# Other groups of query tiles in the index loop of a two-block transformer, VectorE's sums and selections interleaved, one head pair moved behind the loop

## The reference

```python
iq = (hidden_states @ idx_wq_w).reshape(b, s, IDX_H, IDX_D)       # 16 index heads of 128
ik = hidden_states @ idx_wk_w
iw = hidden_states @ idx_weights_w * IDX_H ** (-0.5)
idx_scores = jnp.einsum('bqn,bnqk->bqk', iw, jax.nn.relu(jnp.einsum('bqnd,bkd->bnqk', iq, ik))) * IDX_D ** (-0.5)
idx_scores = jnp.where(causal, idx_scores, -jnp.inf)
_, topk_idx = jax.lax.top_k(idx_scores, TOPK)                     # 128 of up to 1024
...
scores = jnp.where(mask[:, None], scores, -jnp.inf)
attn = jax.nn.softmax(scores, axis=-1)                            # 32 heads
```

## Time and profile before

| | us |
|---|---|
| three runs: median (lowest to highest) | 1416.42 (1415.38 to 1418.27) |
| profiled execution | 1415.27 |
| its span | 1413.5 |
| TensorE busy, of the span | 1308.7 (93%) |
| VectorE busy | 1089.0 (77%) |
| ScalarE busy | 822.2 (58%) |
| GpSimd busy | 715.1 (51%) |

### The profile page before, as it was taken

The page is one execution under the profiler, slowest core; times in us unless marked ns, Lnnn a source line. Parts: engine busy times, 40 slices in busy tenths (PEclk is TensorE's granted clock), DMA queues, the critical chain, the costliest instruction groups (busy, mean ns, idle before and its releaser), DMA issues.

```text
span 1413.5 us, 21378 instructions
## 1 busy us (share of the span) xinstructions
PE 1308.7 (93%) x7147; PEld 1095.1 (77%) x7147; DVE 1089.0 (77%) x2246; ACT 822.2 (58%) x1816; POOL 715.1 (51%) x705
## 2 busy tenths in 40 slices
PE   4868999999899999998689999999999999999998
PEld 3756888888789887876367888888888888888876
DVE  6676334343647798999979889889899989989976
ACT  3653432222246766764567776766677676667761
POOL 3660300010037789984845665565565565566524
PEclk9978999999999999998589999999999999999999
DMA  5640300000212436646620000000000000000021
GB/s 201 208 157 27 118 13 1 1 21 0 70 39 68 125 84 198 209 141 230 207 63 14 24 6 29 29 29 29 29 13 17 29 29 29 29 29 1 16 83 60
DMA packets 83707, 95.53 MB, mean 68 GB/s; under 512 B 11792, under 2 KB 59280, under 8 KB 83088
## 3 DMA queue, kind: packets, MB, share of 16 engines
q1 hardware_dynamic: 83600, 94.17, 20.9%
HBM read 75.27 MB, written 18.87 MB: 67 GB/s over the span
## 4 chain that ended last, share of the span: by engine, by line
PE 73%; DVE 15%; ACT 3%; issue 3%; DMA 2%; POOL 1%; SPq 1%; DVEq 1%; ACTq 0%
PE ps L361 18%; PE ps L362 17%; PE ps L363 17%; PE ps L1986 9%; PE ps L2006 3%; PE ps L2005 3%; DVE rop L1523 1%; DVE xn_l L1573 1%; DVE pm L1553 1%; DVE rop L1521 1%; DVE acc L1498 1%; PE ps L1885 1%; DVE rop L1522 1%; PE ps L1684 1%; DVE top L1511 1%
## 5 line engine op out<-in xcount | busy, mean ns | idle before, releaser
L785 POOL TENSOR_SCALAR pm<-pm,smx 128x128 f32<-128x128 f32 (+1 forms) x255 | 189.3, 751 | 206.5 <-DVE smx L1560 206.4
L1114 ACT ACTIVATE pm<-pm,smx 128x128 f32<-128x128 f32 (+7 forms) x256 | 197.2, 772 | 36.6 <-DVE smx L1553 34.9
L1553 DVE CUSTOM_DVE_ANT_0 pm<-ps,mbias 128x128 f32<-128x128 f32 (+7 forms) x256 | 191.3, 752 | 27.2 <-PE ps L363 12.4
L1986 PE MATMUL ps<-ident,pm 128*128 128x128 f32 x1152 | 174.1, 276 | 7.7 <-DVE xn_l L1573 2.1
L1120 ACT ACTIVATE xn_h<-ps 128x512 fp32r<-128x512 f32 (+3 forms) x256 | 128.7, 513 | 82.1 <-PE ps L1986 79.1
L1573 DVE TENSOR_TENSOR xn_l<-ps,xn_h 128x512 fp32r<-128x512 f32 (+3 forms) x256 | 144.3, 587 | 24.3 <-ACT xn_h L1120 23.2
L1986 PEld LDWEIGHTS ps<-ident,pm 128*128 128x128 f32 x1152 | 134.0, 141 | 33.7 <-issue 11.8
L361 PE MATMUL ps<-latT_l,qc_h 128*128 128x512 f32 (+4 forms) x384 | 142.9, 372 | 16.9 <-DVE smx L1553 8.7
L363 PE MATMUL ps<-latT_h,qc_h 128*128 128x512 f32 (+4 forms) x384 | 132.4, 345 | 0.0
L362 PE MATMUL ps<-latT_h,qc_l 128*128 128x512 f32 (+4 forms) x384 | 132.2, 344 | 0.0
L361 PEld LDWEIGHTS ps<-latT_l,qc_h 128*128 128x128 f32 x384 | 73.2, 191 | 32.6 <-issue 13.1
(11 more groups left out here) (303 smaller groups left out, 3744.7 us busy)
## 6 DMA issues: line engine op xcount, KB each, us to landing
iwq_raw<-in_L_attn_idx_wq_w SPq DMA_DIRECT2D x48, 256.0 KB, 3.0
base<-in_L_ffn_mean_w SPq DMA_DIRECT2D x28, 256.0 KB, 3.4
wring<-in_L_ffn_w SPq DMA_DIRECT2D x21, 256.0 KB, 3.8
ow_raw<-in_L_attn_o_w SPq DMA_DIRECT2D x8, 512.0 KB, 3.9
xn_t<-in_L_attn_o_w SPq DMA_DIRECT2D x8, 512.0 KB, 4.2
wuvo<-pr_even SPq DMA_DIRECT2D x8, 512.0 KB, 5.0
wuvo<-pr_hl SPq DMA_DIRECT2D x8, 512.0 KB, 4.6
wuvo_h<-wuvo SPq DMA_DIRECT2D x16, 256.0 KB, 2.7
```

The lines of the kernel that those rows point to most:

```text
L785: pool.tensor_scalar(pm[:, i % 4, 0:w], pm[:, i % 4, 0:w], smx[:, 32 + i:33 + i], 0.0, ALU.mult, ALU.add).then_inc(hd_p, 1)
L1114: act.activation(pm[:, i % 4, 0:w], pm[:, i % 4, 0:w], ACT.Exp, bias=smx[:, i:i + 1], scale=-1.0, accum_out=smx[:, 16 + i:17 + i]).then_in ...
L1553: dve.tensor_tensor_reduce(out=pm[:, i % 4, 0:w], in0=row_block(2 * (i % 2), t), in1=mbias[:, TRI[t]:TRI[t + 1]], scale=1.0, scalar=3.0 * BIG,
L1986: done = pe.transpose(ps[:, t_bank(p, i), tile(k)], pm[:, tq % 4, tile(4 * c + k)], ident[:])
```

## The change

The groups become tiles (1, 2), (3, 4, 5) and (6, 7). The limit between four and two score slots, and the waits of GpSimd, are now taken from `INDEX_SUMS` (32, 80, 112 sums), so that the four slots are used for tiles 1 and 2 alone. From step 16 on VectorE interleaves: the sum of the first tile, all `max` of a round, the sum of the second tile, all replacements, the sum of a third tile where there is one. `PAIR_AT` holds seven pairs, so `LATER` is 7 and nine pairs follow behind the loop.

```diff
--- before.py
+++ after.py
@@ -57,14 +57,15 @@
 TRI = [P * (t * (t + 1) // 2) for t in range(NT + 1)]
 
 
-INDEX_TILES = ((1, 2, 3), (4, 5), (6, 7))
-INDEX_COLS = ((P, 512), (512, 768), (768, 1024))
+INDEX_TILES = ((1, 2), (3, 4, 5), (6, 7))
+INDEX_COLS = ((P, 384), (384, 768), (768, 1024))
+INDEX_SUMS = (32, 80, 112)
 STEPS = 3 * IDXH
 SPLIT_TILES, SPLIT_COLS = (5, 7), 512
-PAIR_AT = {24: 0, 28: 1, 32: 2, 34: 3, 37: 4, 39: 5, 42: 6, 44: 7}
+PAIR_AT = {27: 0, 33: 1, 35: 2, 37: 3, 39: 4, 42: 5, 44: 6}
 LATER = len(PAIR_AT)
 TAIL_ORDER = [(_step[0], int(_step[1:])) for _step in
-              "P8 F0 F1 P9 F2 F3 P10 P11 M0 P12 L0 M1 P13 L1 M2 P14 L2 P15 M3 L3".split()]
+              "P7 P8 F0 F1 P9 F2 F3 P10 P11 M0 P12 L0 M1 P13 L1 M2 P14 L2 P15 M3 L3".split()]
 TAIL_ACT = {8: "F0 F1", 9: "F2 F3", 11: "E0 E1", 12: "R0 E2", 13: "R1 E3", 14: "R2"}
 LAT_AT = 9
 
@@ -394,13 +395,13 @@
             return [(first + k, t) for k, t in enumerate(tiles)]
 
         def score_bank(n):
-            return 2 + n % 4 if n < 48 else 2 + 2 * (n % 2)
+            return 2 + n % 4 if n < INDEX_SUMS[0] else 2 + 2 * (n % 2)
 
         def score(n, t):
             return row_block(score_bank(n), t)
 
         def slot_free(n):
-            return n - 3 if n < 48 else max(48, n - 1)
+            return n - 3 if n < INDEX_SUMS[0] else max(INDEX_SUMS[0], n - 1)
 
         def acc_of(t):
             return acc[:, TRI[t] - P:TRI[t + 1] - P]
@@ -651,7 +652,7 @@
                                    ALU.subtract).then_inc(ix_w, 1)
 
             def drop_later(phase):
-                pool.wait_ge(ix_acc, (48, 80, 112)[phase])
+                pool.wait_ge(ix_acc, INDEX_SUMS[phase])
                 for t in INDEX_TILES[phase]:
                     d = acc[:, TRI[t] - P + t * P:TRI[t] + t * P]
                     pool.affine_select(out=d, in_=d, compare_op=ALU.is_ge, fill=FUTURE, base=0,
@@ -698,7 +699,7 @@
 
             def topk_mask(phase):
                 for k, t in enumerate(INDEX_TILES[phase]):
-                    pool.wait_ge(tk_rep, (45, 78)[phase] + k + 1)
+                    pool.wait_ge(tk_rep, INDEX_SUMS[phase] - len(INDEX_TILES[phase]) + k + 1)
                     pool.tensor_scalar(mbias[:, TRI[t]:TRI[t + 1]], acc_of(t), TAKEN, BIG, ALU.is_gt, ALU.mult)\
                         .then_inc(tk_mask, 1)
 
@@ -1485,9 +1486,9 @@
                     dve.tensor_tensor(latT_h[KR:P, 1, tile(t)], src[KR:P, P:2 * P],
                                       f(latT_h[KR:P, 1, tile(t)]), ALU.subtract).then_inc(lt_lo, 1)
 
-            def index_sum(step):
+            def index_sum(step, first, last):
                 head, tiles = step % IDXH, index_tiles(step)
-                for n, t in tiles:
+                for n, t in tiles[first:last]:
                     w = iw[:, t, head:head + 1]
                     c = slice(SPLIT_COLS if t in SPLIT_TILES else 0, (t + 1) * P)
                     dve.wait_ge(ix_r, n + 1)
@@ -1498,18 +1499,20 @@
                         dve.scalar_tensor_tensor(acc_of(t)[:, c], score(n, t)[:, c], w, acc_of(t)[:, c],
                                                  ALU.mult, ALU.add).then_inc(ix_acc, 1)
 
-            def topk_round(step):
+            def topk_max(step):
                 tiles = index_tiles(step)
                 for k, (n, t) in enumerate(tiles):
                     if step % IDXH == 0:
                         dve.wait_ge(ix_mask, t + 1)
                         if t in SPLIT_TILES:
                             dve.wait_ge(ix_ga, (SPLIT_TILES.index(t) + 1) * IDXH)
-                        reach(dve, tk_rep, (0, 48, 80)[step // IDXH])
+                        reach(dve, tk_rep, (0, *INDEX_SUMS)[step // IDXH])
                     else:
                         dve.wait_ge(tk_rep, n - len(tiles) + 1)
                     dve.max(top8[:, k, :], acc_of(t)).then_inc(tk_max, 1)
-                for k, (n, t) in enumerate(tiles):
+
+            def topk_replace(step):
+                for k, (n, t) in enumerate(index_tiles(step)):
                     dve.wait_ge(tk_max, n + 1)
                     dve.match_replace(acc_of(t), top8[:, k, :], acc_of(t), TAKEN).then_inc(tk_rep, 1)
 
@@ -1522,13 +1525,19 @@
                 dve.tensor_tensor(rop[lo, i % 2, 1, :], ps[hi, bank, :], sinq[hi, c], ALU.mult)
                 dve.tensor_tensor(rop[hi, i % 2, 1, :], ps[lo, bank, :], sinq[lo, c], ALU.mult).then_inc(hd_rc, 1)
 
-            for step in range(STEPS):
-                index_sum(step)
+            for step in range(IDXH):
+                index_sum(step, 0, None)
                 lat_work(step)
-                if step >= IDXH:
-                    topk_round(step - IDXH)
+            for step in range(IDXH, STEPS):
+                index_sum(step, 0, 1)
+                topk_max(step - IDXH)
+                index_sum(step, 1, 2)
+                topk_replace(step - IDXH)
+                index_sum(step, 2, None)
+                lat_work(step)
             for step in range(2 * IDXH, STEPS):
-                topk_round(step)
+                topk_max(step)
+                topk_replace(step)
             dve.wait_ge(tk_mask, 5)
             dve.wait_ge(hd_go, 1)
```

## The result

| | before | after |
|---|---|---|
| four runs: median (lowest to highest), us | 1417.16 (1415.38 to 1418.27) | 1458.89 (1457.22 to 1459.67) |
| profiled execution, us | 1415.27 | 1457.22 |
| its span | 1413.5 | 1455.4 |

The ratio is 1.0299, with a 95% interval of 1.0285 to 1.0314: the change makes the kernel slower by 42 us. The lines of the kernel after stand 1 to 9 lower in the file than before: the sums are at 1496 and 1499 (before 1495 and 1498), MAX8 at 1512 (1511), the replacements at 1517 (1514), the ReLU at 1000 (999), the first head row at 1562 (1553), the pairs' products at 1894 (1885).

The account below looks back on a forecast made before the run. Two chains ending together, VectorE's selections and the head pairs, were taken to bound the kernel; -16.5 (first third) +27.9 (second) +12.6 (last) +9.7 (ninth pair) = +33.7 us on 1415.27 gave 1449.0, range 1427 to 1461.

Parts of the forecast that it names:

- ring through ScalarE and VectorE: Steps 16 to 31: with two slots tile 5 waits for tile 3 through ScalarE and VectorE; TensorE waits 1.25 us, step 6.05.
- last third: Steps 32 to 47: VectorE binds throughout with the selections of tiles 3, 4, 5; 6.28 us a step, 101.2 in all.
- exposed ninth pair: Tail: one more pair behind the loop costs 8.6 us; the pairs end at 743.6, 11 us behind the selections.
- first third: Steps 0 to 15: fewer columns for TensorE, VectorE's norms 17.1 us; step 16 comes 16.5 us earlier, held to 2.5 us.
- second third: Steps 16 to 31: sixteen steps of 6.05 us and one pair, 100.7 us against 72.8, +27.9.
- its pair: Second third: the one head pair left there lies on TensorE's own path and costs 3.9 us.
- tail to first head: From first tail selection at 662.4 to first head row at 743.6; selections need 70.1 us, then VectorE waits for SP.
- rival 1: Second third: slot waits short or hidden, TensorE paces at 4.7 us; 1428, chance 0.20 with all between 1425 and 1440.
- Rival 2: Loop: TensorE's clock falls; at half clock, +12 us over a quarter of the steps (1461), +50 over all; chance 0.11.
- under 1.00 there: Second third: sign of being wrong, TensorE's granted clock below 1.00.
- Rivals 3 and 4: 3: VectorE keeps the second third's pace, 1409, chance 0.05; 4: pace 4.7 and ninth pair hides, 1418, chance 0.04.

Follow-up runs that it names:

- three slots: Changed kernel with three two-bank score slots in the second third, pairs moved behind it, latent transposes one step earlier: 1439.20 us, ratio 1.0164.
- ReLU first: Changed kernel, two slots kept, with tile 3's ReLU ahead of ScalarE's weight copy in steps 16 to 31: 1451.02 us, ratio 1.0249.
- everything repaired: Changed kernel, groups kept, with three slots, earlier transposes, ReLU first in the second third, VectorE's old order, eight pairs at steps 32 to 46: 1427.50 us, ratio 1.0090.
- seven pairs alone: Kernel before, groups and order old, with seven pairs in the loop at the new places and nine behind it: 1426.37 us, ratio 1.0073.

## Why the prediction was right, and where its sizes were off

**Forecast and mechanism.** 1449.0 us was forecast for the profiled execution, 1457.22 measured; the median, 1458.89, lies within 1427 to 1461, but above the 1440 to 1457 that had the chance of 0.60. The nearness is in part luck. Between step 0 and the first head 33.7 us more were forecast and 46.3 came, 12.6 too few; 4.4 of them were made good by a start 2.8 us earlier and by 1.6 us behind the first head, and neither was in the sum. The forecast mechanism happened: two slots, a ring through ScalarE and VectorE, a VectorE-bound last third, an exposed ninth pair. Each also answered to its own experiment (three slots and ReLU first; everything repaired; seven pairs alone). That the last third's cost comes from VectorE's moved work rests on its busy row and on the last run together, not on a run that changes it alone.

| term, us | forecast | measured |
|---|---|---|
| first third | 46.9 | 54.0 |
| second third | 100.7 | 103.0 |
| a step in it | 6.05 | 6.19 |
| its pair | 3.9 | 4.0 (103.0 - 16 x 6.19) |
| last third | 101.2 | 101.95 |
| a step in it | 6.28 | 6.27 |
| tail to first head | 81.2 | 83.7 |

**First third: the term that failed, by 7.1 us.** I held it to 2.5 us. Steps 0 to 8 took 29.6 us where I had worked out 23.9 (413.58 to 437.5), and three things make up the difference. I carried the norms over as fixed work, and their instructions took 2.5 us longer (see the last section). I let VectorE wait for nothing, and it waited 2.4 us, 2.0 of them at once for a ReLU. I took off 0.7 us for an earlier start of step 0, which does not shorten this stretch. The engine that I left out is GpSimd: it was busy for 11.4 of the 12 us from 416 to 428, and TensorE stood for its low part of the queries, here and once more by 1.24 us:

```profile
419.14 0.39 PE L362 MATMUL ps<-ikT_l,iqT_h 128*128 128x256 f32 x1 [1.89 <-POOL iqT_l L678]
```

Steps 8 to 16 took 24.4 us, not 23.0. (The numbers of the prediction add up to 437.4 and 460.2, not 437.5 and 460.5.) Some 1.0 of the 1.4 us goes with the clock. Five profiled versions with this first third have 0.79 of full speed between 432 and 448 us and take 24.3 to 24.6 us for these steps; the one with seven pairs and VectorE's old order, which is no different here, has 0.89 and takes 23.4. First the changed kernel, then that one:

```profile
432.00:448.00 16.00, 12.54 (x78) 12.36 (x78) 12.61 (x28) 7.99 (x22) 8.46 (x10) 0.79 0.23 66
```

```profile
432.00:448.00 16.00, 12.28 (x85) 11.75 (x84) 13.61 (x30) 8.96 (x25) 9.46 (x11) 0.89 0.23 67
```

One step of 3.3 us adds to it, in which GpSimd makes the halves of the latent values (`v`) first and TensorE waits for the low part of the queries behind them:

```profile
447.07 0.36 PE L362 MATMUL ps<-ikT_l,iqT_h 128*128 128x256 f32 x1
...
450.39 0.39 PE L362 MATMUL ps<-ikT_l,iqT_h 128*128 128x256 f32 x1 [0.50 <-POOL iqT_l L678]
```

```profile
448.38 1.28 POOL L698 TENSOR_TENSOR v<-latn,v 128x512 fp32r<-128x512 f32 x1
449.61 0.72 POOL L678 TENSOR_TENSOR iqT_l<-iq_f,iqT_h 128x256 fp32r<-128x256 f32 x1
```

I had taken the work away from TensorE and not asked which engine that work used to hide, the very argument I used one third later.

**Second third: right to 2.3 us.** The wait was put at 1.25 us and is 1.20; the ReLU was put 1.48 us behind the projection's end and starts there (493.60 to 495.08). Tile 5 takes 1.15 instead of 1.05 and the projection 2.13 instead of 2.09: the first matmul behind a wait starts the next 0.33 us later, where one without a wait takes 0.22 to 0.24. That VectorE's new order changes nothing in this third held: undone, the steps are the same. The pair was put at 3.9 us without a working, and 4.0 came, but some 1.5 of them are a slower clock in the step behind it: with VectorE's old order and the clock at 1.00 the pair cost 2.4.

**Last third: right to 0.8 us.** Three rows, from one step's sum of tile 6 to the next one's, with no idle time ahead of any:

```profile
575.11 1.14 DVE L1499 SCALAR_TENSOR_TENSOR acc<-ps,iw,acc 128x896 f32<-128x896 f32 x1
576.17 2.27 DVE L1512 MAX8 top<-acc 128x8 f32<-128x512 f32 x3
...
581.38 1.15 DVE L1499 SCALAR_TENSOR_TENSOR acc<-ps,iw,acc 128x896 f32<-128x896 f32 x1
```

**Tail: 2.5 us short.** The place was right (the wait ends with SP, and is 13.6 us where 11 were forecast), the price was not: the stores, bounded at 0 to 4 us, were taken as 0, and nothing was said of the queries, which move with `LATER` as well and stand 5.2 us. No run says how the 2.5 us divide between the two.

**Rivals.** TensorE's pace of 4.7 us in the second third was rival 1, and it is what the kernel does with three slots; at two the ReLU's place decides, as written. Rival 2, the clock, put +12 us on a quarter of the steps. It came true on a small scale. The second third shows 0.98 (by the letter of "under 1.00 there" a sign of being wrong), and that is one place: TensorE waited 1.97 us, its longest wait there, and 1.2 GHz followed for some 3 us.

```profile
543.66 0.49 PE L362 MATMUL ps<-ikT_l,iqT_h 128*128 128x512 f32 x1 [1.97 <-DVE acc L1499]
```

```profile
544.00:548.00 4.00, 4.00 (x17) 3.91 (x16) 2.49 (x7) 1.84 (x3) 1.29 (x1) 0.61 0.23 66
```

It made the next step 7.72 us long instead of 6.19. With the 1.0 us of the first third the clock cost some 2.5 us, a fifth of what the rival asked. By the rule of the Trainium skill that I weighed (TensorE: Matmul & The Clock Gate, "Part 1: The HAM clock gate") a TensorE with waits might have fallen back; with waits of 1.2 us, one a step, the trace shows that it did not, and behind the longer one that it did.

Rivals 3 and 4 fell: the pace would have had to be under 3.95 or at 4.7, and was 6.19. (By the terms of the prediction rival 3 ends the pairs at 702.7 us, not 704, and the kernel at 1408.)

## What to carry to other kernels

When buffers get fewer or wider, lay out the ring from a producer over every engine back to the same buffer, with whatever stands ahead of each step in its engine's order: no engine was full here, and mending the ring gave 19 us. When one tile of work moves between stages, price it by what binds in the stage that receives it, and ask of the stage that gets shorter which engine or wait its length had been hiding. When a loop count such as `LATER` moves, list everything that is keyed to it, on each engine and in each queue.

## What the hardware showed unasked

**VectorE's small instructions next to GpSimd.** The same instructions of the latent norms sum to 20.0 us of busy time in the changed kernel and to 17.5 before. First the changed kernel, the Newton steps on 128x16 elements, and GpSimd's rows at the time:

```profile
424.80 0.68 DVE L1164 TENSOR_TENSOR rs_tmp<-rs_out 128x16 f32<-128x16 f32 x1
425.55 1.16 DVE L1166 TENSOR_TENSOR rs_tmp<-rs_tmp,rs_var 128x16 f32<-128x16 f32 x1
```

```profile
424.72 0.73 POOL L678 TENSOR_TENSOR iqT_l<-iq_f,iqT_h 128x256 fp32r<-128x256 f32 x1 [0.16 <-issue]
425.40 1.28 POOL L651 TENSOR_TENSOR iwq_l<-iwq_raw,iwq_h 128x512 fp32r<-128x512 f32 x1
```

Then the second of them in the kernel before, where it starts between two of GpSimd's instructions:

```profile
432.03 0.17 DVE L1165 TENSOR_TENSOR rs_tmp<-rs_tmp,rs_var 128x16 f32<-128x16 f32 x1
```

0.17 us or 1.16 for the same instruction: it ends at 426.71, with GpSimd's, at 426.68. The Trainium skill (SBUF — State Buffer, "Who interferes with whom") says that a VectorE instruction with two inputs in SBUF and a GpSimd instruction that reads SBUF exclude each other for the whole of whichever came first; these rows agree. That the 2.5 us of the norms came from it was not tested by a run of its own.

**What a late sum does to the clock.** In the same place VectorE's norms kept one sum back, TensorE stood 3.46 us, and its clock fell from 0.96 in 432 to 436 us to 0.50 (1.2 GHz throughout) and 0.69 (1.2 GHz for part of the time) behind it, though TensorE was busy again:

```profile
432.00:436.00 4.00, 1.05 (x9) 0.84 (x8) 4.00 (x6) 1.65 (x5) 3.62 (x4) 0.96 0.46 131
436.00:440.00 4.00, 3.49 (x15) 3.52 (x16) 3.91 (x13) 0.84 (x2) 0.00 (x0) 0.50 0.22 66
440.00:444.00 4.00, 4.00 (x25) 4.00 (x25) 2.31 (x5) 2.31 (x6) 1.98 (x2) 0.69 0.00 0
```

The waits of 1.2 us, one a step, left the clock at 1.00; the one of 3.46 us did not, nor did the one of 1.97 us in the second third. But a wait alone does not settle it: in the version with seven pairs and VectorE's old order TensorE waited the same 1.97 us at 543.86, and its clock stayed at 1.00 over the whole second third. What decides between the two is open.
